# Perceiver block on one core: the end of a batch with its norm turned one batch later, statistics behind the normalisation, and the queries' low part and the norm on GpSimd

## What is computed

```python
x = x + xattn(layernorm(x), ctx, mask, W_q, W_k, W_v, W_o, b_o)   # x [8,128,512], ctx [8,2048,384], 8 heads of 64
x = x + attn(layernorm(x), Wq, Wkv, Wo)                           # h as [L=8, B=128, 512], 16 heads of 64
x = x + ffn(layernorm(x), w_gate, w_up, w_down)                   # ternary weights, 8-bit activations, inner size 2048
```

## Time and profile before

| what | us |
|---|---|
| median of 3 runs | 760.68 |
| lowest and highest run | 758.98, 764.14 |
| the profiled execution, its whole time | 762.53 |
| its span, first to last instruction | 758.9 |
| busy in the span: TensorE, VectorE, ScalarE, GpSimd | 671.7, 437.4, 356.4, 106.8 |

### The profile page before, as it was taken

One profiled execution on the slowest core, in us unless ns is written; L12 is line 12 of the kernel. 1 busy time (PEld: TensorE's weight loads), 2 busy tenths in 40 slices (PEclk: granted clock), 3 DMA queues, 4 the chain that ended last, 5 costly groups with the idle time before them and its releaser, 6 DMA issues.

```text
span 758.9 us, 14299 instructions
## 1 busy us (share of the span) xinstructions
PE 671.7 (89%) x4244; PEld 526.3 (69%) x4244; DVE 437.4 (58%) x960; ACT 356.4 (47%) x846; POOL 106.8 (14%) x143
## 2 busy tenths in 40 slices
PE   3988689979799779979879989999999899889996
PEld 2768568868688658868768767777777678535453
DVE  5523444454544444445567766666666444699974
ACT  3333334434334323444410166666666343578984
POOL 2590000010100110010100012222222100012121
PEclk9998899989889798979979999999999899999999
DMA  8000000000000000004159844444454333000111
GB/s 319 24 24 23 24 2 22 22 21 22 2 22 22 21 2 21 23 21 146 65 205 305 299 160 151 156 156 156 160 167 165 128 125 125 1 1 15 28 28 41
DMA packets 40067, 64.91 MB, mean 86 GB/s; under 512 B 4056, under 2 KB 20440, under 8 KB 40032
## 3 DMA queue, kind: packets, MB, share of 16 engines
q1 hardware_dynamic: 40032, 64.45, 25.2%
HBM read 53.95 MB, written 10.49 MB: 85 GB/s over the span
## 4 chain that ended last, share of the span: by engine, by line
PE 70%; issue 10%; DVE 9%; POOL 4%; DVEq 3%; ACT 3%; ACTq 0%; POOLq 0%
PE bank L588 40%; PE bank L724 6%; PE bank L957 6%; PE bank L712 3%; PE bank L697 3%; PE bank L965 2%; PE bank L872 2%; DVE tern L1661 2%; POOL x_all L514 1%; PE bank L849 1%; PE bank L907 1%; PE bank L860 1%; ACT cxT_hi L1058 1%; DVE wqk_odd_lo L1371 1%; DVE h_f L1766 1%
## 5 line engine op out<-in xcount | busy, mean ns | idle before, releaser
L1075 ACT ACTIVATE probs<-probs,negm 128x256 f32<-128x256 f32 x104 | 52.1, 501 | 88.2 <-DVE negm L1475 87.6
L1475 DVE CUSTOM_DVE_ANT_0 probs<-bank,bias,negm_old 128x256 f32<-128x256 f32 x104 | 46.0, 480 | 43.5 <-PE bank L697 43.5
L957 PE MATMUL bank<-w_T,xqT 128*128 128x512 bf16 x256 | 58.4, 379 | 4.7 <-ACT xqT L1260 2.0
L724 PEld LDWEIGHTS bank<-v_sb,pT 128*128 128x128 f32 x416 | 52.3, 191 | 5.5
L485 POOL TENSOR_TENSOR rstd<-var_eps,neg_half 128x1 f32 (+1 forms) x16 | 10.0, 625 | 325.1 <-DVE var_eps L1538 252.5
L1371 DVE TENSOR_TENSOR kT_lo<-bank,kT_hi 128x512 fp32r<-128x512 f32 x28 | 19.4, 693 | 62.4 <-ACT kT_hi L1064 62.4
L724 PE MATMUL bank<-v_sb,pT 128*128 128x64 f32 x416 | 54.7, 274 | 0.0
L1068 ACT COPY v_sb<-bank 128x512 f32<-128x512 f32 x28 | 15.2, 590 | 76.5 <-PE bank L724 73.5
L697 PE MATMUL bank<-kT_hi,qT_hi 64*128 64x256 f32 x104 | 22.9, 430 | 30.9 <-issue 27.7
L957 PEld LDWEIGHTS bank<-w_T,xqT 128*128 128x128 bf16 x256 | 24.1, 98 | 34.9 <-issue 2.9
L588 PE MATMUL bank<-cxT_hi,wk_hi 128*128 128x256 f32 x168 | 39.3, 349 | 4.6 <-ACT cxT_hi L1058 4.5
(11 more groups left out here) (236 smaller groups left out, 1695.8 us busy)
## 6 DMA issues: line engine op xcount, KB each, us to landing
tern_dram<-tern SPq DMA_DIRECT2D x8, 768.0 KB, 5.3
tstage<-tern_dram SPq DMA_DIRECT2D x8, 768.0 KB, 4.2
cx<-in_ctx_dram SPq DMA_DIRECT2D x14, 384.0 KB, 3.0
absw<-in_L_ffn_w_gate_dram SPq DMA_DIRECT2D x8, 512.0 KB, 3.9
absw<-in_L_ffn_w_up_dram SPq DMA_DIRECT2D x8, 512.0 KB, 5.3
absw<-in_L_ffn_w_down_dram SPq DMA_DIRECT2D x8, 512.0 KB, 6.5
tern_raw<-in_L_ffn_w_gate_dram SPq DMA_DIRECT2D x8, 512.0 KB, 6.0
tern_raw<-in_L_ffn_w_up_dram SPq DMA_DIRECT2D x8, 512.0 KB, 6.8
```

Of the source, the lines that this page charges most:

```text
L724: last = mm(bank[7][:, h * DH:(h + 1) * DH], pT[:, g % 2, at:at + P], v_sb[:, t, h * DH:(h + 1) * DH], start=(t == 0), stop=(t == CT - 1))
L957: last = mm(bank[3 + 2 * which + c % 2][:], xqT[:, u, k * P:(k + 1) * P], w_T[:, which, k, c * 512:c * 512 + 512], start=(k == 0), stop=(k ...
L1075: fn(probs[:, h, :], probs[:, h, :], ACT.Exp, bias=negm[:, h:h + 1], scale=-1.0, accum_out=csum[:, h:h + 1]).then_inc(p_done, 1)
L1475: nc.vector.tensor_tensor_reduce(probs[:, h, :], bank[3 + h % 2][:, 0:CHUNK], bias[:], -SCALE, negm_old[:, h:h + 1], ALU.add, ALU.min, neg ...
```

## The change

At the end of a batch the statistics now stand behind `normalise`; the norm is made by GpSimd in two passes (subtract the mean, multiply by the reciprocal root, a settling instruction ahead of each), and it is turned and split at the next batch's end, ahead of `project_output`. The queries' low part moves to GpSimd, for the first batch between the bias adds and the clearing. Behind the loop `turn_norm(B - 3)` is added ahead of the last projection; the last batch's norm has a buffer (`xn_last`, the place of `on_c`) and a bank (5) of its own and stays, with batch 6's, on VectorE; the low parts of `wv2` are made behind all norms, and the values' first two groups run the two terms without them first.

```diff
             def query_low(b):                      # GpSimd
+                pool.wait_ge(qT_hi, START + b + 1)
+                settle_p()
+                nc.gpsimd.tensor_tensor(qT.lo[:], qT_all[:, :, bass.ds(within(b) * P, P)], f32(qT.hi[:]), ALU.subtract).then_inc(qT_lo, 1)
+
+            def norm(b):
+                pool.wait_ge(rstd_c, START + b + 1)
+                pool.wait_ge(lnT_ps, START + b)
+                settle_p()
+                nc.gpsimd.tensor_tensor(xn_c[:], tile_of(x_all, b), mv[:, 0, 0:1].broadcast_to([P, D]), ALU.subtract).then_inc(xn_centred, 1)
+                pool.wait_ge(xn_centred, START + b + 1)
+                settle_p()
+                nc.gpsimd.tensor_tensor(xn_c[:], xn_c[:], rstd[:, bass.ds(within(b), 1)].broadcast_to([P, D]), ALU.mult).then_inc(xn_p_done, 1)
...
+            query_low(0)
             pool.wait_ge(qT_ps, START + 2 * DK)
             nc.gpsimd.memset(o_all[:], 0.0).then_inc(zeroed, 1)
...
             with pool.Fori(1, B - 1) as b:
+                with pool.If(b < B - 2):
+                    query_low(b + 2)
                 rsqrt(b - 1, var_c, rstd_c)
+                norm(b - 1)
                 residual(b)
...
                 pe.wait_ge(negm_done, START + H * chunks)
+                with pe.If(b > 2):
+                    turn_norm(b - 3)
                 with pe.If(b > 0):
                     project_output(b - 1)
                 turn_output(b)
-                with pe.If(b > 1):
-                    turn_norm(b - 2)
+            turn_norm(B - 3)
             project_output(B - 1)
             turn_norm(B - 2)
-            turn_norm(B - 1)
+            turn_norm_last()
...
+            for g in range(2):
+                second_values(g, 0, (0, 1))
+                second_values(g, 1, (0, 1))
+            for g in range(2):
+                second_values(g, 0, (2,))
+                second_values(g, 1, (2,))
...
                     query_high(b + 1, act.snap(done))
+                with act.If(b > 2):
+                    norm_high(b - 3)
                 with act.If(b > 0):
                     projected(b - 1)
                 output_high(b)
-                with act.If(b > 1):
-                    norm_high(b - 2)
...
-                with dve.If(b > 1):
-                    norm_stats(b - 2)
                 normalise(b, chunks)
-                with dve.If(b > 1):
-                    norm(b - 2)
                 with dve.If(b < B - 1):
-                    query_low(b + 1)
+                    unseen(b + 1)
+                with dve.If(b > 1):
+                    dve.wait_ge(xn_p_done, START + b - 2)
+                    norm_stats(b - 2)
+                with dve.If(b > 2):
+                    norm_low(b - 3)
                 output_low(b)
-                with dve.If(b > 1):
-                    norm_low(b - 2)
...
+            norm_low(B - 3)
+            dve.wait_ge(xn_p_done, START + B - 2)
             norm_stats(B - 2)
-            values_low(0)
             residual_last()
             norm_stats(B - 1, 1)
             norm(B - 2)
-            values_low(1)
-            norm(B - 1, 1)
+            norm_last()
             norm_low(B - 2)
-            values_low(2)
-            norm_low(B - 1)
-            values_low(3)
+            norm_low(B - 1, 5)
+            for k in range(DK):
+                values_low(k)
```

More of the change, by code:

```diff
@@ L133, in bass_perceiver_block_kernel @@
         on_c = at("on_c", 162, D)
+        xn_last = on_c
         o_all = at("o_all", 164, B, D)
@@ L813, in _, with second_values @@
-            pe.wait_ge(lnT_hi, START + B)
-            for g in range(G):
-                if g >= 2:
-                    pe.wait_ge(v2_act, START + g - 1)
-                    pe.wait_ge(v2_dve, START + g - 1)
+            turn_norm_last()
+            VALUE2_TERMS = (("hi", "hi"), ("lo", "hi"), ("hi", "lo"))
+            def second_values(g, half, terms=(0, 1, 2)):
+                for i in terms:
+                    a, c = VALUE2_TERMS[i]
+                    for k in range(DK):
+                        if g == 0 and half == 0:
+                            if a == "lo" and k == 0:
+                                pe.wait_ge(lnT_lo, START + B)
+                            elif c == "lo":
+                                pe.wait_ge(wv2_lo, START + k + 1)
+                            elif a == "hi":
+                                pe.wait_ge(wv2_hi, START + k + 1)
+                        last = mm(bank[2 * (g % 2) + half][:], part(ln_T, a)[:, k, g * P:(g + 1) * P],
+                                  part(wv2, c)[:, k, half * 512:half * 512 + 512],
+                                  start=(i == 0 and k == 0), stop=(i == 2 and k == DK - 1))
+                if 2 in terms:
+                    last.then_inc(v2_ps, 1)
@@ L1543, in norm, with unseen @@
                 ts(xn_c[:], tile_of(x_all, b), mv[:, slot, 0:1], rstd[:, bass.ds(within(b), 1)], ALU.subtract, ALU.mult).then_inc(xn_c_done, 1)
-            def query_low(b):
-                dve.wait_ge(qT_hi, START + b + 1)
-                low(qT.lo[:], qT_all[:, :, bass.ds(within(b) * P, P)], qT.hi[:]).then_inc(qT_lo, 1)
+            def unseen(b):
                 nc.vector.memset(negm_old[:], UNSEEN).then_inc(unseen_done, 1)
@@ L1551, in _ @@
                 context_low(0, piece)
-            query_low(0)
+            unseen(0)
             dve.wait_ge(w_lo, START + 3)
```

68 lines of the change are left out of this document (41 added, 27 removed).

## The result

| | before | changed |
|---|---|---|
| median (6 runs each), us | 759.83 | 753.2 |
| lowest, highest | 758.25, 764.14 | 749.69, 755.96 |
| ratio, 95% interval | | 0.9899, 0.9853 to 0.9944 |
| profiled execution, its span | 762.53, 758.9 | 755.63, 753.6 |

The forecast was 758.8 us, with a range from 753.5 to 765.5. A second set of six runs gave 751.07 and a ratio of 0.9889 (0.9843 to 0.9936).

What follows compares the result with a forecast made beforehand. VectorE was taken to bound the seven batch ends, TensorE most of the rest. Loop -8.2, start +1.1 and end +5.2 sum to -1.9 us, from the 760.68 median to 758.8; range 753.5 to 765.5 for 8 of 10.

Steps and rivals of the forecast that it cites:

- the loop's term: At the seven batch ends the gap from last sum to next `probs` shrinks, 8.2 us saved in all (6.0 to 9.5).
- The reading of the bound: At batch ends the chain runs through VectorE; the time from the last sum to its last low part can be saved.
- the collisions: At batch ends `qT_lo`, and in batch 5 `xn_c`, are held beside GpSimd's residual add, taking 1.76 and 1.60 us.
- The statistics' place alone: At batch ends, statistics standing ahead of `on_c` delay it by 1.1 us; the change puts them behind it.
- The start: Before the first `probs`, GpSimd's low part of the first queries adds 1.1 us net, between 0.8 and 1.8.
- The tail: Behind the loop, the last projection waits for GpSimd's norm of batch 5, adding 5.2 us (3.2 to 6.8).
- the end costs nothing: Rival: after the loop the loads catch up, so the projection's delay costs nothing; 753.6 us, chance 0.12.
- The rival "`on_c` held": At batch ends GpSimd takes the SBUF interface first and holds `on_c`; 4.1 us slower, 764.8 us, chance 0.20.

Runs made afterwards that it cites:

- second: Changed kernel with the queries' low part back on VectorE, behind the normalisation and ahead of the statistics, the first batch's pass too; 751.88 us.
- third experiment: Changed kernel with the statistics ahead of the reciprocal and `on_c` again; 754.75 us.
- fourth: Changed kernel with GpSimd's clearing of `o_all` and `l_all` placed ahead of the first queries' low part; 751.0 us.
- fifth: Changed kernel with two unused reductions of bank 5 added on VectorE between the wait for `onT_hi` and the last low part; 755.44 us.
- sixth experiments: Changed kernel with the norm moved from GpSimd's two passes back to VectorE's one, still turned a batch later; 753.58 us (12 runs).
- first experiment: Changed kernel with the last projection placed ahead of the last turn of GpSimd's norm in TensorE's list; 751.77 us.

## Why the prediction was wrong

**The step that failed is the loop's term:** "The gap becomes 4.7 + 3.8 = 8.5; I take 8.6, since two lists end there together." The 3.8 was right: from the start of `onT_lo` to `probs` it is 203.62 - 199.82 = 3.80. The 4.7, at which `onT_lo` was to start, is 4.36. TensorE's four transposes, for which I took 0.7, put the work behind them later by 0.36: the next group starts at 195.62, 0.36 behind their start at 195.26, though the row gives them 0.61, and `onT_hi` ends at +4.33 against +3.97 at ends without them. The 0.1 for two lists that end together was not there either: the low part ahead of `onT_lo` on VectorE ends at +4.00, and 0.69 more in that list changed nothing. So batches 3, 4 and 6 gained 1.59 on average instead of 1.15 and batch 5 2.86 instead of 2.4. Batch 2 gained 2.01 instead of 1.9, batch 1 0.20 as forecast, and batch 0 0.53 instead of 0.2, because TensorE's branches set that gap: its last transposes end 0.25 sooner, and it takes 3.49 instead of 3.77 from there to the scores. That makes -10.4 where I had -8.2, with -9.5 as its end.

**The reading of the bound failed as well,** though it hardly moved the sum, which counted to the start of `onT_lo`. "What can be saved is the time from the last sum into `o_all` to that last low part", and "Two things make up the 1.8 to 3.0 us above batch 1", the statistics and the collisions: both look at VectorE's instructions. The time to save was that up to VectorE's last wait: at the ends of batches 2 to 6 before that for `ln_T_hi` (its end at +5.67 in batch 2, and 4.13 from there to `probs`), now that for `onT_hi`. VectorE's engine time had no say here: neither 0.69 more ahead of `onT_lo` nor 1.2 more behind the wait moved a gap. The Trainium skill, "Perfetto Trace Analysis", section "DVE / Act Engine Instruction (TENSOR_ADD, Activation, etc)", has the sequencer free for the next instruction as soon as one is pushed into the wait queue. The traces agree that it runs ahead of the engine; here, though, the branches followed only once the wait was met (0.06 in the chain), so the measurement narrows the rule.

**What the parts of the change give** came out otherwise than the prediction's working. The statistics' place alone, for which I took 1.1 per end as a saving, made the kernel slower. The later turn alone brings the gaps from 9.75 to 8.65; with it in place the statistics' place is what the last half microsecond, to 8.16, rests on: with queries and norm on GpSimd it is 9.00 with the statistics ahead of `on_c` (0.28 of it the collision) and 8.16 with them behind it. With queries and norm on VectorE only the statistics ahead were run (8.64). The queries on GpSimd give nothing, and the norm there gives 0.3 in batch 2, 0.1 in batch 5 and nothing else.

**The start** was right: 0.82 in 0.8 to 1.8. The order on GpSimd is its cause: with the clearing first, `probs` comes at 58.65, 0.55 ahead of the kernel before, so the pass ahead of the clearing costs 1.37 (forecast 1.5) and the collision that is gone gives back 0.55 (forecast 0.4).

**The tail** was right in its mechanism and too large: the wait is 3.04 as forecast (some 3), the projection came 2.10 later against its batch instead of 5.2. The root started at +3.40 instead of +3.8, GpSimd's passes took 1.04 instead of 1.3, and the clock stayed full in this profile. It need not: of the seven profiles with such a wait, 1.65 to 3.04 us (the changed kernel twice, and the second, third, fourth, fifth and sixth experiments), three ran the projection at the full clock, two at 0.67 and two at 0.52 or 0.53. "I take 5.2, nearer the slow end" was a fair middle, but a profile gets one of them. The second values, which the prediction put some 3 later, start at +15.20, before at +15.41. The loads did not catch up, as the earlier trace rows let expect: at the means' product the delay was 4.0, and 3.2 in the second profile. The DMA queue waits 1.7 for the projection (2.3 before) and 4.6 for the last tile's store (4.3), and the sums' idle time for DMA is 10.7 now, 9.4 before. So "the end costs nothing" does not hold, as the first experiment shows, which got 3.5 us back. That its 753.6 lies next to the measured 753.2 is chance: the tail's loss is there, and the larger gain in the loop and the rows without a term make up for it. The errors add up: loop -2.2, tail -1.2 (4.0 against 5.2), start -0.3, and -1.3 for what had no term in my sum and is partly scatter, the first chunks, the stretch behind the means and the time outside the span (-1.25, +1.51, -1.60). That is -5.0, the distance of 755.63 from the 760.6 that the prediction gave for this execution.

**The rival "`on_c` held"** does not occur, because `on_c` ends at 197.28, before GpSimd's pass starts at 197.37; where the third experiment brought them together it cost up to 0.28.

## What to carry to other kernels

Where an engine's list ends in branches, look in the chain for how long it stays in the last instruction: if that is far below the instruction's duration, the time may run from the last wait that the sequencer met. Work on the engine then counts only where it delays that wait, or where it outlasts the branches: here 0.69 more ahead of the last low part and 1.2 more behind the wait cost nothing, with 3.10 of cover. Ask of every reordering which wait will be met last, on each list, and move the instruction that others need (a turn, a cast) rather than the one that takes long. Of a move to an idle engine, look at the ends of the loop first: here the two moves to GpSimd gave 0.4 us in the loop and cost 0.8 at the start and 0.9 of TensorE's wait at the end (3.04 against 2.11 with the norm on VectorE), where its slower passes stood alone on the path.

## What the runs showed of the hardware

- VectorE's branches ran beside its own unfinished instructions: `onT_lo` ended at +5.05, +5.33 or +6.25 and the next `probs` came at +8.16 or +8.17 each time.
- GpSimd's pass of 128x512 with a column broadcast took 1.04, that of the queries' low part, with two full tensors, 1.26 to 1.30.
- VectorE's `xn_c`, with one full tensor, was held beside GpSimd's add as well (1.23 and 1.37 for 0.55), while the statistics beside GpSimd's pass kept their 0.69.
- The granted clock behind the same silence of 3.0 us was full in some executions and at its low level in others, and the first chunk of a batch, which in batches 1 to 7 stands behind the gap, took between 17.6 and 19.9 us. Two executions of the end of batch 1, each after a gap of 7.80, in the view by windows of TensorE (us, busy time, granted clock, the DMA engines' busy share and GB/s); the changed kernel, chunk of 18.92:

```profile
113.59:117.00 3.41, 2.95 (x16) 0.50 0.39 112
117.00:121.00 4.00, 4.00 (x28) 0.76 0.01 3
```

and the kernel with VectorE kept busy, chunk of 17.59:

```profile
113.51:117.00 3.49, 3.10 (x20) 0.73 0.32 113
117.00:121.00 4.00, 4.00 (x37) 1.00 0.00 0
```

The runs of one kernel spread over 2.7 to 9.8 us; this scatter of the clock is a part of it that the profiles show, and how much of it was not measured.
